# Attention on one Trainium2 core: 128-wide matmuls placed between wide ones, P in two buffers

## The chip, the core and the metric

The kernel runs on one core of one Trainium2 chip. The metric is the device time of one execution in microseconds, median of the runs. The engines have short names here: PE is TensorE's matmul side and PEld its weight loads, DVE is VectorE, ACT is ScalarE, POOL is GpSimd, SP issues DMAs. TensorE's clock has two levels, 1.2 and 2.4 GHz; the granted clock is shown as a share of the upper one.

## The reference, cut to what matters

```python
def attn(x, W_K, W_Q, W_V, W_O):        # x 4 x 512 x 256, 16 heads of 128
    k = einsum('ihd,bpd->biph', W_K, x)
    q = einsum('ihd,bpd->biph', W_Q, x)
    v = einsum('ihd,bpd->biph', W_V, x)
    scores = einsum('biph,biqh->biqp', k, q)
    mask = tril(ones((pos, pos)))
    masked = scores * mask - 1e10 * (1.0 - mask)
    attn = softmax(masked / sqrt(d_head), axis=-1)
    z = einsum('biqp,biph->biqh', attn, v)
    return einsum('df,bqf->bqd', W_O, z_flat)
...
mod = (silu(c) @ wmod).reshape(4, 6, 1, -1)         # sa, ca, ga, sb, cb, gb
h = layernorm(x) * (1 + ca) + sa
x = x + ga * attn(h, ...)
h = layernorm(x) * (1 + cb) + sb
x = x + gb * ffn(h, ...)     # down 256->128, top-2 of 8 experts, shared expert, up, core path
```

The change touches the attention, and of the rest only where the vector gb is kept.

## The kernel before

All is fp32. Nearly every operand of a matmul is kept as two parts in the rounded type fp32r, a high part and a low part, and each product is three matmuls in a row: high by high, high by low, low by high (`mm3`, L631 to L633). Each matmul loads its own 128x128 stationary operand.

The attention is cut into 64 units, one for each batch element and head (`unit(u)`). A unit has these steps on PE. The steps q and k project to 128 x 512, six 512-wide matmuls each. The step v is twelve 256-wide matmuls. S makes the causal scores in twelve matmuls: four row blocks i, each 128(i+1) wide, three matmuls per block. T transposes the ten 128x128 blocks of the normalised scores P on PE (L733). The step z multiplies the transposed P by v in twelve matmuls that are 512, 384, 256 and 128 wide, three of each. The step wo is the output projection, twelve 256-wide matmuls.

Between these steps work the other engines. For S, DVE adds the mask and takes the row minimum of the negated scores (nb, L1034), ACT takes exp into PB and sums rows (L535), DVE takes the reciprocals (ri, L1043), and then ACT scales the last row block (L574) and DVE the other three (L1047, "norm"). For T, ACT copies each bank's transposes to `pth` (L597) and DVE makes the low part `ptl` (L1054); T uses the banks T0, T1 and S2, and z waits until all three low parts are made (`s_pl`). For q, k, v and z, ACT copies the high part (L586) and DVE makes the low part (L1023); their results and wo's go through the three banks M0 to M2 in turn.

One list of steps, `attention_plan()`, sets the order on every engine: each engine walks the same list and does its own share of each step, strictly in that order, so a step's place in the list is its place in ACT's and DVE's queues as well. In the steady part an iteration i is: S(i+1), q(i+2), k(i+2), norm(i+1), wo, z(i), one v, T(i+1). The exps of S(i+1) are split in ACT's queue: those of the first bank stand at S, those of the other two behind the copy of q(i+2). "fill" steps (layer norms, router) are put between. After the attention `ffn_plan()` runs the feed-forward part in the same way; its first gelu, step dn(0), is asked on ACT to wait for the last T (L602), since its result lies where PB was.

Of the kernel before, what the change touches and what calls it, by code (L numbers as in the profile page):

```python
# [13 lines left out]
NU = B * H  # L14
# [33 lines left out]
def attention_plan():  # L48
# [20 lines left out]
    for b in range(2):  # L69
# [14 lines left out]
            ("nm", 0, 0), ("nm", 0, 1), ("mod",),  # L84
            ("h", 0, 0), ("h", 0, 1), ("wh", 2), ("q", 0), ("k", 0), ("v", 0, 0), ("S", 0), ("norm", 0), ("q", 1), ("k", 1), ("v", 0, 1), ("T", 0), ("wh", 3)]
    for i in range(NU):
        steps = list(fill.get(i, []))

        def add(*events):
            for ev in events:  # L90
                plan.append(ev)
                if steps and ev[0] in ("S", "q", "wo", "z", "v", "T"):
                    plan.extend(steps.pop(0))

        if i + 1 < NU:
            add(("S", i + 1))
        if i + 2 < NU:
# [12 lines left out]
        plan += post.get(i, [])  # L110
        if i + 2 == NU:
            plan.append(("dn", 0))
# [85 lines left out]
def build(nc, x, ct, wmod, wat, wfa, wfb, cst, bcol, b2, ub, cb, out, scr, scw):  # L198
# [20 lines left out]
    with ExitStack() as ctx:  # L219
# [12 lines left out]
        cc = sb("cc", C_END)  # L232
        gab = sb("gab", 2048)
        bc = sb("bc", B_END)
# [43 lines left out]
        s_x = [sem(f"s_x{b}") for b in range(B)]  # L278
        s_ct, s_wm, s_wm2, s_c, s_b, s_bc, s_g = (sem(n) for n in ("s_ct", "s_wm", "s_wm2", "s_c", "s_b", "s_bc", "s_g"))
        s_st = [sem("s_st0"), sem("s_st1")]  # L280
# [21 lines left out]
        def bank(ev):  # L302
            return M[use[ev] % 3]

        def hT(b, k):
# [71 lines left out]
        def _(sp):  # L377
# [12 lines left out]
            for ev in plan:  # L390
# [4 lines left out]
                elif ev[0] == "wh":  # L395
# [30 lines left out]
        def _(pool):  # L426
# [7 lines left out]
            for ev in plan:  # L434
# [6 lines left out]
                if ev[0] == "mg":  # L441
# [16 lines left out]
                    pool.wait_ge(s_gd, 32)  # L458
                    flat = scr.rearrange("(o a) b n -> o (a b n)", o=1)
                    pool.dma_start(gab[:], flat.broadcast_to([128, 2048])).then_inc(s_g, 16)  # L460
                if ev[0] == "acc" and ev[2] > 0 and ev not in OWN:
# [36 lines left out]
                if ev[0] == "xb":  # L498
# [5 lines left out]
                    pool.wait_ge(s_xn, 2 * (B + t) + 2)  # L504
                    pool.wait_ge(s_g, 16)
                    pool.tensor_tensor(gob[:], oub[:], g, ALU.mult).then_inc(s_xb, 1)
# [13 lines left out]
        def _(act):  # L520
# [5 lines left out]
            def exps(u, ns):  # L526
                for n in ns:
# [4 lines left out]
                    for i in chunks:  # L532
                        w = 128 * (i + 1)
                        a = S_AT[i][1]
                        ins = act.activation(PB[:, P_OFF[i]:P_OFF[i] + w], PS[bk][:, a:a + w], ACT.Exp,  # L535
                                             bias=nb[:, i:i + 1], scale=-1.0, accum_out=sm[:, i:i + 1])
                    ins.then_inc(s_E, 1)

            for ev in plan:
# [30 lines left out]
                elif kind == "norm":  # L570
                    u = ev[1]
                    act.wait_ge(s_ri, u + 1)
                    p = PB[:, P_OFF[3]:P_OFF[3] + 512]
                    act.activation(p, p, ACT.Copy, scale=ri[:, 3:4]).then_inc(s_P3, 1)  # L574
# [54 lines left out]
        def _(pe):  # L629
            def mm3(o, lhs, rhs, start, stop, **kw):  # L630
                pe.matmul(o, lhs[0], rhs[0], start=start, stop=False, **kw)  # L631
                pe.matmul(o, lhs[0], rhs[1], start=False, stop=False, **kw)  # L632
                return pe.matmul(o, lhs[1], rhs[0], start=False, stop=stop, **kw)  # L633

            pe.wait_ge(s_z, 1)
# [7 lines left out]
            for ev in plan:  # L643
# [42 lines left out]
                elif kind in ("q", "k"):  # L686
# [6 lines left out]
                    for k in range(2):  # L693
                        if k and h == 0:
                            pe.wait_ge(me, use[("h", b, 1)] + 1)
                        ins = mm3(o[:], wt(g % 2, a + 512 * k, 128), hT(b, k), k == 0, k == 1)
                    ins.then_inc(mf, 1)
                elif kind == "v":
# [8 lines left out]
                elif kind == "S":  # L707
# [6 lines left out]
                    for n, (bk, chunks) in enumerate(S_ORDER):  # L714
                        if u > 0:
                            pe.wait_ge(s_E, 3 * u - 3 + n + 1)
                            if bk == 2:
                                pe.wait_ge(s_pl, 3 * u - 2)
                        for i in chunks:
                            a, w = S_AT[i][1], 128 * (i + 1)  # L720
                            ins = mm3(PS[bk][:, a:a + w], lane(q, 128 * i, 128), lane(kk, 0, w), True, True)
                        ins.then_inc(s_S, 1)
                elif kind == "T":
                    u = ev[1]
                    pe.wait_ge(s_N, u + 1)
                    pe.wait_ge(s_P3, u + 1)
                    for n, (bk, chunks) in enumerate(T_ORDER):
                        if u > 0:
                            pe.wait_ge(s_pl, 3 * u - 3 + n + 1)
                        for j in chunks:  # L730
                            a = T_AT[j]
                            for i in range(j, 4):
                                ins = pe.transpose(PT[bk][:, a + 128 * (i - j):a + 128 * (i - j) + 128],  # L733
                                                   PB[:, P_OFF[i] + 128 * j:P_OFF[i] + 128 * j + 128], ident)
                        ins.then_inc(s_T, 1)
                elif kind == "z":
# [4 lines left out]
                    pe.wait_ge(s_pl, 3 * u + 3)  # L741
                    for j in range(4):
                        w = 512 - 128 * j
                        ins = mm3(o[:, 128 * j:512], (vh[:, va + 256 * j:va + 256 * j + 128],
                                                      vl[:, va + 256 * j:va + 256 * j + 128]),
                                  (pth[:, T_OFF[j]:T_OFF[j] + w], ptl[:, T_OFF[j]:T_OFF[j] + w]), j == 0, j == 3)
                    ins.then_inc(mf, 1)
# [102 lines left out]
        def _(v):  # L850
# [81 lines left out]
            for ev in plan:  # L932
# [105 lines left out]
                elif kind == "norm":  # L1038
# [6 lines left out]
                    for i in (1, 0, 2):  # L1045
                        p = PB[:, P_OFF[i]:P_OFF[i] + 128 * (i + 1)]
                        ins = v.tensor_scalar(p, p, ri[:, i:i + 1], None, ALU.mult)  # L1047
# [136 lines left out]
                elif kind == "up":  # L1184
                    _, t, c2 = ev
                    v.wait_ge(mf, use[ev] + 1)
                    if t:
                        v.wait_ge(s_fin, 2 * t - 1 + c2)
                    fbuf = fb[:, 512 * c2:512 * c2 + 512]
                    f = fbuf.rearrange("p (a n) -> p a n", a=2)  # L1190
                    g = gab[:, 1024 + t * 256:1280 + t * 256].rearrange("p (a n) -> p a n", a=1)
                    v.tensor_tensor(f, bank(ev)[:].rearrange("p (a n) -> p a n", a=2), bcast(g, [128, 2, 256]),
                                    ALU.mult).then_inc(me, 1)
# [65 lines left out]
```

## Time and profile before

| | |
|---|---|
| three timed runs | 903.02, 901.08, 902.13 us; median 902.13 |
| span of the profiled execution | 901.1 us |
| PE busy | 872.9 us (97%), 5462 matmuls |
| PEld busy | 781.2 us (87%) |
| DVE, ACT, POOL busy | 76%, 62%, 30% |
| mean granted clock | 0.980 |

The profiled execution is known by its span, the time from the first to the last instruction; nothing is listed outside it. The start of a matmul in a timeline is recorded, its end is modelled: matmuls are pipelined, so their durations overlap and the distance between two starts is the time that one takes of the engine. In brackets behind a row stands how long the engine was idle before it, and on whose result it waited. The chain that ended last lies on PE for 83% of the span.

### The profile page before, as it was taken

What the parts mean: (1) busy time and instruction counts of PE and PEld (TensorE: products, weight loads), DVE (VectorE), ACT (ScalarE), POOL (GpSimd) and SP (SyncE); (2) the same over time, 40 slices, a digit from 0 to 9 for tenths busy, and PEclk for the clock granted to TensorE, in tenths of its full rate; (3) what the DMA queues carried; (4) which work ended last, traced back from release to release, by engine and by line L of the source; (5) the groups of instructions that cost most, each with busy time, mean ns of one, the idle gap of its engine ahead of it and who ended that gap; (6) DMA issues with size and microseconds to landing.
All of it is one profiled execution on the core that took longest, in us unless ns stands there. A gap on an engine that the chain in (4) does not pass through costs nothing.

```text
span 901.1 us, 15397 instructions
## 1 busy us (share of the span) xinstructions
PE 872.9 (97%) x5462; PEld 781.2 (87%) x5462; DVE 689.2 (76%) x1705; ACT 563.0 (62%) x1274; POOL 268.3 (30%) x183
## 2 busy tenths in 40 slices
PE   6999999999999999999999999999999998999996
PEld 6889999999999999999999999999999875777675
DVE  5778887777777777777777777778788979687996
ACT  3655766566566656655665665666656677485772
POOL 3142222211112221111222211232141465577753
PEclk7999999999999999999999999999999999799998
DMA  7120000000000010000000000010000020112130
GB/s 243 47 95 1 24 25 24 24 1 1 2 1 24 24 27 22 1 1 1 25 24 24 24 1 1 24 42 24 2 1 1 26 74 22 58 48 83 47 103 27
DMA packets 10442, 28.63 MB, mean 32 GB/s; under 512 B 1408, under 2 KB 1568, under 8 KB 10112
## 3 DMA queue, kind: packets, MB, share of 16 engines
q1 hardware_dynamic: 9712, 25.80, 9.0%
q0 software_dynamic: 368, 1.34, 0.4%
q8 instruction: 44, 0.72, 0.3%
q10 hardware_dynamic: 288, 0.53, 0.2%
q14 instruction: 30, 0.25, 0.1%
HBM read 25.49 MB, written 2.17 MB: 31 GB/s over the span
## 4 chain that ended last, share of the span: by engine, by line
PE 83%; DVE 7%; issue 3%; ACT 3%; POOL 2%; DMA 1%; POOLq 0%; DVEq 0%; ACTq 0%
PE M L631 18%; PE M L632 18%; PE M L633 18%; PE T L733 6%; PE S L631 6%; PE S L633 5%; PE S L632 5%; DVE Gr L1182 3%; PE S L733 2%; PE T L631 1%; PE T L632 1%; PE T L633 1%; ACT G L623 1%; ACT Gr L625 1%; DMA bc<-in_bcol 1%
## 5 line engine op out<-in xcount | busy, mean ns | idle before, releaser
L489 POOL TENSOR_TENSOR X<-X,fb 128x512 f32<-128x512 f32 x64 | 83.5, 1305 | 521.9 <-DVE fb L1068 521.9
L535 ACT ACTIVATE PB<-S,nb 128x128 f32<-128x128 f32 (+3 forms) x256 | 133.9, 534 | 117.5 <-DVE nb L1034 117.5
L1023 DVE TENSOR_TENSOR qk<-M,qk 128x512 fp32r<-128x512 f32 x128 | 88.4, 692 | 82.2 <-ACT qk L586 82.2
L1034 DVE CUSTOM_DVE_ANT_0 S<-S,cc 128x128 f32<-128x128 f32 (+3 forms) x256 | 117.6, 522 | 0.6 <-PE S L633 0.6
L631 PE MATMUL M<-hh,W 128*128 128x512 f32 x264 | 104.7, 397 | 2.3 <-DVE hl L1010 2.3
L632 PE MATMUL M<-hl,W 128*128 128x512 f32 x264 | 104.1, 394 | 0.0
L633 PE MATMUL M<-hh,W 128*128 128x512 f32 x264 | 103.7, 393 | 0.0
L1182 DVE TENSOR_TENSOR Gr<-G,Gr 128x512 fp32r<-128x512 f32 x84 | 81.0, 972 | 19.7 <-ACT Gr L625 19.1
L631 PE MATMUL S<-qk 128*128 128x128 f32 (+3 forms) x256 | 88.1, 344 | 0.0
L623 ACT ACTIVATE G<-S,bc 128x512 f32<-128x512 f32 x84 | 58.1, 691 | 48.0 <-PE S L633 34.4
L633 PE MATMUL M<-pth,vl 128*128 128x512 f32 (+3 forms) x256 | 82.8, 324 | 0.0
L632 PE MATMUL M<-ptl,vh 128*128 128x512 f32 (+3 forms) x256 | 82.6, 323 | 0.0
L633 PE MATMUL S<-qk 128*128 128x128 f32 (+3 forms) x256 | 82.4, 322 | 0.0
L632 PE MATMUL S<-qk 128*128 128x128 f32 (+3 forms) x256 | 82.2, 321 | 0.0
L1054 DVE TENSOR_TENSOR ptl<-T,pth 128x512 fp32r<-128x512 f32 x128 | 81.9, 681 | 0.1
L586 ACT CAST qk<-M 128x512 fp32r<-128x512 f32 x128 | 76.1, 595 | 7.0 <-PE M L633 7.0
L574 ACT ACTIVATE PB<-PB,ri 128x512 f32<-128x512 f32 x64 | 46.3, 724 | 53.9 <-DVE ri L1043 53.9
L631 PE MATMUL M<-pth,vh 128*128 128x512 f32 (+3 forms) x256 | 79.3, 310 | 0.0
L1023 DVE TENSOR_TENSOR vl<-M,vh 128x512 fp32r<-128x512 f32 x64 | 44.3, 691 | 42.4 <-ACT vh L586 42.2
L631 PE MATMUL M<-W,hh 128*128 128x256 f32 x256 | 75.4, 295 | 0.0
L633 PE MATMUL M<-W,hl 128*128 128x256 f32 x256 | 72.5, 283 | 0.0
L632 PE MATMUL M<-W,hh 128*128 128x256 f32 x256 | 72.3, 282 | 0.0
(186 smaller groups left out, 2484.3 us busy)
## 6 DMA issues: line engine op xcount, KB each, us to landing
stage<-in_wat SPq DMA_DIRECT2D x16, 512.0 KB, 3.9
gab<-scw SPq DMA_DIRECT2D x16, 256.0 KB, 3.3
tmp<-scw SPq DMA_DIRECT2D x16, 256.0 KB, 3.4
X<-in_x SPq DMA_DIRECT2D x4, 512.0 KB, 6.0
stage<-in_wfa SPq DMA_DIRECT2D x3, 512.0 KB, 3.8
out<-X SPq DMA_DIRECT2D x3, 512.0 KB, 2.6
X<-in_wmod SPq DMA_DIRECT2D x1, 1024.0 KB, 7.7
gab<-scr POOLq DMA_DIRECT2D x1, 1024.0 KB, 5.0
```

Source lines behind the costliest of these rows:

```text
L489: pool.tensor_tensor(X[:, a:a + 512], X[:, a:a + 512], fb[:, c2 * 512:c2 * 512 + 512], ALU.add).then_inc(s_y, 1)
L535: ins = act.activation(PB[:, P_OFF[i]:P_OFF[i] + w], PS[bk][:, a:a + w], ACT.Exp, bias=nb[:, i:i + 1], scale=-1.0, accum_out=sm[:, i:i + 1])
L586: act.copy(dst, bank(ev)[:]).then_inc(mh, 1)
L623: act.activation(G32[:, (n % 2) * 512:(n % 2) * 512 + 512], PS[n % 3][:], ACT.Gelu, bias=bias).then_inc(s_v, 1)
L631: pe.matmul(o, lhs[0], rhs[0], start=start, stop=False, **kw)
L632: pe.matmul(o, lhs[0], rhs[1], start=False, stop=False, **kw)
L633: return pe.matmul(o, lhs[1], rhs[0], start=False, stop=stop, **kw)
L733: ins = pe.transpose(PT[bk][:, a + 128 * (i - j):a + 128 * (i - j) + 128], PB[:, P_OFF[i] + 128 * j:P_OFF[i] + 128 * j + 128], ident)
L1023: v.tensor_tensor(lo, bank(ev)[:], hi.bitcast(F32), ALU.subtract).then_inc(me, 1)
L1034: ins = v.tensor_tensor_reduce(PS[bk][:, a:a + w], PS[bk][:, a:a + w], mask[:, 512 - w:512], -INV, BIG, ALU.add, ALU.min, nb[:, i:i + 1])
L1054: v.tensor_tensor(ptl[:, a:z], PT[bk][:, 0:z - a], pth[:, a:z].bitcast(F32), ALU.subtract).then_inc(s_pl, 1)
L1182: v.tensor_tensor(lo, G32[:, (n % 2) * 512:(n % 2) * 512 + 512], hi.bitcast(F32), ALU.subtract).then_inc(s_gl, 1)
```

## The change

Four things are changed in the attention.

1. The ten transposes of unit i no longer stand together. Each of the first five 512-wide matmuls of q(i+2) and of k(i+2) is followed by one of them (`t_step`), in the order bank T0 (4), T1 (4), S2 (2).
2. In S the three products of the 384-wide and the 128-wide block alternate, and in z those of the 512-wide and the 128-wide block. S now starts with bank S2.
3. P has two buffers, by the parity of the unit: PB and a new stretch of `gab`. The vector gb, which was there, is loaded by a DMA of its own after the last T.
4. In the list T(i) stands behind k(i+2) and ahead of norm(i+1), and v now stands ahead of z. ACT's copies and DVE's low parts of T(i) move with it. For the last two units there is no q or k, and T stands in one piece right ahead of z.

```diff
-S_ORDER = [(1, [0, 2]), (0, [3]), (2, [1])]
+S_ORDER = [(2, [1]), (1, [2, 0]), (0, [3])]
-T_ORDER = [(2, [2]), (1, [1, 3]), (0, [0])]
+T_ORDER = [(0, [0]), (1, [1, 3]), (2, [2])]
+T_STEPS = [(bk, j, i) for bk, js in T_ORDER for j in js for i in range(j, 4)]
...
         if i + 2 < NU:
             add(("q", i + 2), ("k", i + 2))
-        if i + 1 < NU:
-            add(("norm", i + 1))
-        if i >= 2:
-            add(("wo", i // 2 - 1, i % 2))
+            add(("T", i), ("norm", i + 1))
+            add(("wo", i // 2 - 1, i % 2)) if i >= 2 else None
+        else:
+            add(("wo", i // 2 - 1, i % 2), ("T", i))
+            add(("norm", i + 1)) if i + 1 < NU else None
         add(*pre.get(i, []))
-        add(("z", i))
         if i + 2 < NU:
             add(("v", i // 2 + 1, i % 2))
-        if i + 1 < NU:
-            add(("T", i + 1))
+        add(("z", i))
...
+        def P_at(u, a, n):
+            return PB[:, a:a + n] if u % 2 == 0 else gab[:, 1024 + a:1024 + a + n]
...
+                elif ev == ("z", NU - 1):
+                    sp.wait_ge(s_gd, 32)
+                    sp.wait_ge(s_T, 3 * NU)
+                    flat = scr[1].rearrange("(o b) n -> o (b n)", o=1)
+                    sp.dma_start(gab[:, 1024:2048], flat.broadcast_to([128, 1024])).then_inc(s_gb, 16)
...
+            def t_step(u, n):
+                bk, j, i = T_STEPS[n]
+                if n == 0:
+                    pe.wait_ge(s_N, u + 1)
+                    pe.wait_ge(s_P3, u + 1)
+                if n in (0, 4, 8) and u > 0:
+                    pe.wait_ge(s_pl, 3 * u - 3 + n // 4 + 1)
+                if n == 8 and u + 1 < NU:
+                    pe.wait_ge(s_E, 3 * (u + 1) + 1)
+                a = T_AT[j] + 128 * (i - j)
+                ins = pe.transpose(PT[bk][:, a:a + 128], P_at(u, P_OFF[i] + 128 * j, 128), ident)
+                if n in (3, 7, 9):
+                    ins.then_inc(s_T, 1)
...
-                        ins = mm3(o[:], wt(g % 2, a + 512 * k, 128), hT(b, k), k == 0, k == 1)
-                    ins.then_inc(mf, 1)
+                        w, h_ = wt(g % 2, a + 512 * k, 128), hT(b, k)
+                        for n, (l, r) in enumerate(((0, 0), (0, 1), (1, 0))):
+                            ins = pe.matmul(o[:], w[l], h_[r], start=(k == 0 and n == 0), stop=(k == 1 and n == 2))
+                            if (k, n) == (1, 2):
+                                ins.then_inc(mf, 1)
+                            if ev[1] >= 2 and 3 * k + n < 5:
+                                t_step(ev[1] - 2, 5 * (kind == "k") + 3 * k + n)
...
+                        for m_, (l, r) in enumerate(((0, 0), (0, 1), (1, 0))):
+                            for i in chunks:
+                                a, w = S_AT[i][1], 128 * (i + 1)
+                                ins = pe.matmul(PS[bk][:, a:a + w], lane(q, 128 * i, 128)[l], lane(kk, 0, w)[r],
...
+                    for n in range(10 if ev[1] + 2 >= NU else 0):
+                        t_step(ev[1], n)
...
+                    for js in ((0, 3), (1,), (2,)):
+                        for m_, (l, r) in enumerate(((vh, pth), (vh, ptl), (vl, pth))):
+                            for j in js:
+                                ins = pe.matmul(o[:, 128 * j:512], l[:, va + 256 * j:va + 256 * j + 128],
```

On PE in the steady part, before: the end of a v (M<-W,hl and the like), the ten transposes (T<-cc,PB), and the start of S (S<-qk). The names are output<-inputs.

```order
L632 MATMUL M<-W,hh 128x256
L633 MATMUL M<-W,hl 128x256
L733 MATMUL S<-cc,PB 128x128 x2
L733 MATMUL T<-cc,PB 128x128 x8
L631 MATMUL S<-qk 128x128
L632 MATMUL S<-qk 128x128
L633 MATMUL S<-qk 128x128
L631 MATMUL S<-qk 128x384
```

After the change, the end of S and the start of q(i+2):

```order
L751 MATMUL S<-qk 128x512 x3
L722 MATMUL M<-hh,W 128x512
L655 MATMUL T<-cc,PB 128x128
L722 MATMUL M<-hl,W 128x512
L655 MATMUL T<-cc,PB 128x128
L722 MATMUL M<-hh,W 128x512
L655 MATMUL T<-cc,PB 128x128
L722 MATMUL M<-hh,W 128x512
```

The transposes left the place ahead of S and stand one by one behind 512-wide matmuls (M<-hh,W and M<-hl,W).

On ACT in the steady part, before: copies of z and v, copies of the transposes (pth), exps of the first bank (PB,sm<-S,nb), copy of q, the other exps, copy of k.

```order
L586 CAST zt<-M 128x512 [waits mf]
L586 CAST vh<-M 128x512 [waits mf]
L597 CAST pth<-S 128x256 [waits s_T]
L597 CAST pth<-T 128x512 [waits s_T] x2
L535 ACTIVATE PB,sm<-S,nb 128x128 [waits s_N,s_M]
L535 ACTIVATE PB,sm<-S,nb 128x384
L586 CAST qk<-M 128x512 [waits mf]
L535 ACTIVATE PB,sm<-S,nb 128x512 [waits s_M]
L535 ACTIVATE PB,sm<-S,nb 128x256 [waits s_M]
L586 CAST qk<-M 128x512 [waits mf]
```

After the change, from the first bank's exp to the copies of the transposes:

```order
L544 ACTIVATE gab,sm<-S,nb 128x256 [waits s_N,s_M]
L595 CAST qk<-M 128x512 [waits mf]
L544 ACTIVATE gab,sm<-S,nb 128x384 [waits s_M]
L544 ACTIVATE gab,sm<-S,nb 128x128
L544 ACTIVATE gab,sm<-S,nb 128x512 [waits s_M]
L595 CAST qk<-M 128x512 [waits mf]
L606 CAST pth<-T 128x512 [waits s_T] x2
L606 CAST pth<-S 128x256 [waits s_T]
L583 ACTIVATE gab<-gab,ri 128x512 [waits s_ri]
```

The copies of the transposes stood between the copy of v and the exps; now they stand behind the copy of k, and the exps behind the copy of q are those of the 384-, 128- and 512-wide blocks.

On ACT at the end of the attention, before: the last T's copies, then the first gelus of the feed-forward part (u, ur), then the copy of the last z.

```order
L586 CAST zt<-M 128x512 [waits mf]
L597 CAST pth<-S 128x256 [waits s_T]
L597 CAST pth<-T 128x512 [waits s_T] x2
L605 ACT_TABLE_LOAD [waits s_T]
L605 ACTIVATE u<-M,bc 128x512 [waits mf]
L607 ACTIVATE ur<-M,bc 128x512
L586 CAST zt<-M 128x512 [waits mf]
```

After the change:

```order
L583 ACTIVATE gab<-gab,ri 128x512 [waits s_ri]
L595 CAST zt<-M 128x512 [waits mf]
L614 ACT_TABLE_LOAD [waits s_T]
L614 ACTIVATE u<-M,bc 128x512 [waits mf]
L616 ACTIVATE ur<-M,bc 128x512
L606 CAST pth<-T 128x512 [waits s_T] x2
L606 CAST pth<-S 128x256 [waits s_T]
L595 CAST zt<-M 128x512 [waits mf]
```

The load of gelu's table, which waits for the last T on PE (s_T), and both gelus now stand ahead of the copies of that T.

## Rows read from the trace of the kernel before

**Rows 1.** Busy time and granted clock (PEclk) by stretch: the attention's steady part.
```profile
205.00:600.00 395.00, 395.00 (x2635) 366.53 (x2634) 288.67 (x754) 243.97 (x609) 74.97 (x49) 1.00 0.05 14
```

**Rows 2.** Timeline of PE over one unit: start, duration in us, operation, shapes.
```profile
303.48 0.30 PE L631 MATMUL S<-qk 128*128 128x128 f32 x1
...
305.48 0.40 PE L631 MATMUL M<-hh,W 128*128 128x512 f32 x1
...
308.22 0.28 PE L631 MATMUL M<-W,zt 128*128 128x256 f32 x1
...
312.87 0.28 PE L633 MATMUL M<-W,hl 128*128 128x256 f32 x1
...
314.00 0.30 PE L631 MATMUL S<-qk 128*128 128x128 f32 x1
```

**Rows 3.** Timeline at the end of z's narrow matmuls: matmuls (PE) and weight loads (PEld).
```profile
311.23 0.19 PEld L632 LDWEIGHTS M<-ptl,vh 128*128 128x128 f32 x1
...
311.45 0.19 PEld L631 LDWEIGHTS M<-W,hh 128*128 128x128 f32 x1
311.51 0.33 PE L631 MATMUL M<-W,hh 128*128 128x256 f32 x1
311.56 0.19 PEld L632 LDWEIGHTS M<-W,hh 128*128 128x128 f32 x1
311.68 0.28 PE L632 MATMUL M<-W,hh 128*128 128x256 f32 x1
```

**Rows 4.** Timeline of PEld: the transposes' loads and the first load of S.
```profile
302.58 0.90 PEld L733 LDWEIGHTS T<-cc,PB 128*128 128x128 f32 x8
303.45 0.19 PEld L631 LDWEIGHTS S<-qk 128*128 128x128 f32 x1
```

**Rows 5.** Timeline around a matmul that waited for DVE.
```profile
104.52 0.69 DVE L1010 TENSOR_TENSOR hl<-fb,hh 128x512 fp32r<-128x512 f32 x1 [0.37 <-ACT hh L569]
...
105.26 0.19 PEld L631 LDWEIGHTS M<-hh,W 128*128 128x128 f32 x1 [0.29 <-DVE hl L1010]
...
105.37 0.19 PEld L632 LDWEIGHTS M<-hl,W 128*128 128x128 f32 x1
105.60 0.40 PE L632 MATMUL M<-hl,W 128*128 128x512 f32 x1
```

**Rows 6.** Timeline of ACT between scores and the copy of q.
```profile
316.84 0.37 ACT L535 ACTIVATE PB<-S,nb 128x128 f32<-128x128 f32 x1 [1.81 <-DVE nb L1034]
...
317.76 0.58 ACT L586 CAST qk<-M 128x512 fp32r<-128x512 f32 x1
318.22 0.71 ACT L535 ACTIVATE PB<-S,nb 128x512 f32<-128x512 f32 x1
...
318.90 0.49 ACT L535 ACTIVATE PB<-S,nb 128x256 f32<-128x256 f32 x1
```

**Rows 7.** Timeline at a hand-over from PE to ACT to DVE.
```profile
323.39 0.28 PE L633 MATMUL M<-W,hl 128*128 128x256 f32 x1
...
323.71 0.59 ACT L586 CAST vh<-M 128x512 fp32r<-128x512 f32 x1 [0.90 <-PE M L633]
...
324.33 0.69 DVE L1023 TENSOR_TENSOR vl<-M,vh 128x512 fp32r<-128x512 f32 x1 [0.79 <-ACT vh L586]
...
324.94 0.41 DVE L1054 TENSOR_TENSOR ptl<-S,pth 128x256 fp32r<-128x256 f32 x1
```

**Rows 8.** Timeline of DVE: evictions of the transposes back to back.
```profile
314.75 1.28 DVE L1054 TENSOR_TENSOR ptl<-T,pth 128x512 fp32r<-128x512 f32 x2
315.94 0.29 DVE L1034 CUSTOM_DVE_ANT_0 S<-S,cc 128x128 f32<-128x128 f32 x1
```

**Rows 9.** Waits of PE: total us, times, longest.
```profile
PE S L733 <- DVE PB L1047: 3.0, 2, 1.6
```

**Rows 10.** Timeline of ACT at the end of the attention.
```profile
707.59 1.28 ACT L605 ACT_TABLE_LOAD   x1
...
709.47 0.68 ACT L607 ACTIVATE ur<-M,bc 128x512 fp32r<-128x512 f32 x1
```

More of the change, by code:

```diff
@@ L84, in attention_plan @@
             ("nm", 0, 0), ("nm", 0, 1), ("mod",),
[L85 removed]
+            ("h", 0, 0), ("h", 0, 1), ("wh", 2), ("q", 0), ("k", 0), ("v", 0, 0), ("S", 0), ("norm", 0), ("q", 1), ("k", 1), ("v", 0, 1), ("wh", 3)]
     for i in range(NU):
@@ L232, in build @@
         cc = sb("cc", C_END)
-        gab = sb("gab", 2048)
+        gab = sb("gab", 1024 + 1280)
         bc = sb("bc", B_END)
@@ L278, in build @@
         s_x = [sem(f"s_x{b}") for b in range(B)]
-        s_ct, s_wm, s_wm2, s_c, s_b, s_bc, s_g = (sem(n) for n in ("s_ct", "s_wm", "s_wm2", "s_c", "s_b", "s_bc", "s_g"))
+        s_ct, s_wm, s_wm2, s_c, s_b, s_bc, s_g, s_gb = (sem(n) for n in ("s_ct", "s_wm", "s_wm2", "s_c", "s_b", "s_bc", "s_g", "s_gb"))
         s_st = [sem("s_st0"), sem("s_st1")]
@@ L458, in _ @@
                     pool.wait_ge(s_gd, 32)
-                    flat = scr.rearrange("(o a) b n -> o (a b n)", o=1)
-                    pool.dma_start(gab[:], flat.broadcast_to([128, 2048])).then_inc(s_g, 16)
+                    flat = scr[0].rearrange("(o b) n -> o (b n)", o=1)
+                    pool.dma_start(gab[:, 0:1024], flat.broadcast_to([128, 1024])).then_inc(s_g, 16)
                 if ev[0] == "acc" and ev[2] > 0 and ev not in OWN:
@@ L504, in _ @@
                     pool.wait_ge(s_xn, 2 * (B + t) + 2)
-                    pool.wait_ge(s_g, 16)
+                    pool.wait_ge(s_gb, 16)
                     pool.tensor_tensor(gob[:], oub[:], g, ALU.mult).then_inc(s_xb, 1)
@@ L534, in exps @@
                         a = S_AT[i][1]
-                        ins = act.activation(PB[:, P_OFF[i]:P_OFF[i] + w], PS[bk][:, a:a + w], ACT.Exp,
+                        ins = act.activation(P_at(u, P_OFF[i], w), PS[bk][:, a:a + w], ACT.Exp,
                                              bias=nb[:, i:i + 1], scale=-1.0, accum_out=sm[:, i:i + 1])
@@ L572, in _ @@
                     act.wait_ge(s_ri, u + 1)
-                    p = PB[:, P_OFF[3]:P_OFF[3] + 512]
+                    p = P_at(u, P_OFF[3], 512)
                     act.activation(p, p, ACT.Copy, scale=ri[:, 3:4]).then_inc(s_P3, 1)
@@ L716, in _ @@
                             pe.wait_ge(s_E, 3 * u - 3 + n + 1)
[L717 to L721, printed above, removed]
+                            if bk == 2 and u > 1:
+                                pe.wait_ge(s_pl, 3 * u - 3)
+                        for m_, (l, r) in enumerate(((0, 0), (0, 1), (1, 0))):
+                            for i in chunks:
+                                a, w = S_AT[i][1], 128 * (i + 1)
+                                ins = pe.matmul(PS[bk][:, a:a + w], lane(q, 128 * i, 128)[l], lane(kk, 0, w)[r],
+                                                start=(m_ == 0 and i == chunks[0]), stop=(m_ == 2),
+                                                skip_group_check=True)
                         ins.then_inc(s_S, 1)
                 elif kind == "T":
[L724 to L735, printed above, removed]
+                    for n in range(10 if ev[1] + 2 >= NU else 0):
+                        t_step(ev[1], n)
                 elif kind == "z":
@@ L741, in _ @@
                     pe.wait_ge(s_pl, 3 * u + 3)
[L742 to L746, printed above, removed]
+                    for js in ((0, 3), (1,), (2,)):
+                        for m_, (l, r) in enumerate(((vh, pth), (vh, ptl), (vl, pth))):
+                            for j in js:
+                                ins = pe.matmul(o[:, 128 * j:512], l[:, va + 256 * j:va + 256 * j + 128],
+                                                r[:, T_OFF[j]:T_OFF[j] + 512 - 128 * j],
+                                                start=(j == 0 and m_ == 0), stop=(j == 2 and m_ == 2),
+                                                skip_group_check=True)
                     ins.then_inc(mf, 1)
@@ L1045, in _ @@
                     for i in (1, 0, 2):
-                        p = PB[:, P_OFF[i]:P_OFF[i] + 128 * (i + 1)]
+                        p = P_at(u, P_OFF[i], 128 * (i + 1))
                         ins = v.tensor_scalar(p, p, ri[:, i:i + 1], None, ALU.mult)
@@ L1191, in _ @@
                     g = gab[:, 1024 + t * 256:1280 + t * 256].rearrange("p (a n) -> p a n", a=1)
+                    if t == 0 and c2 == 0:
+                        v.wait_ge(s_gb, 16)
                     v.tensor_tensor(f, bank(ev)[:].rearrange("p (a n) -> p a n", a=2), bcast(g, [128, 2, 256]),
```

## Prediction

> **What bounds the kernel now.** I looked first at the busy times by stretch. Between 205 and 600 us PE is busy for all 395 us at the full clock [rows 1], and no wait of PE falls in that stretch. So a unit costs what its matmuls take of PE. The timeline of PE then gives the unit: from one S to the next it is 314.00 - 303.48 = 10.52 us [rows 2]. The reader is to take distances between starts there, not durations. A 512-wide matmul takes (308.22 - 305.48)/12 = 0.228 us; from 311.68 [rows 3] to 312.87 [rows 2] are ten 256-wide ones, 0.119 us each.
>
> The 128-wide ones are the special case. Their matmuls would need a quarter of 0.228, but their weight loads start 0.11 us apart (311.23, two later 311.45) [rows 3], and the eight transposes' loads take (303.45 - 302.58)/8 = 0.109 us each [rows 4]. They are bound by the load. What can a wide neighbour hide of that? The end of z tells. The 256-wide matmul behind the narrow ones is recorded at 311.51, and its successor comes at 311.68, 0.17 us later instead of 0.12. The successor's load starts at 311.56. Another case says the same: a 512-wide matmul that had waited has its load at 105.26, the next load at 105.37 and the next matmul at 105.60 [rows 5]. The distance of 0.34 is 0.11 for its own load and 0.23 for its stream. I read from both that a matmul truly begins when its load is through, 0.11 us after it started, and that the next load starts just then and not earlier. Then every matmul costs the longer of its own stream and its successor's load, whatever stands next to it.
>
> **The change on PE.** There are 16 128-wide matmuls in a unit (10 in T, 3 in S, 3 in z). By this rule each costs 0.11 us before and after: alone behind a wide one, its own load was hidden before as well, but the load of the wide one that follows can't start before it does. The gain of the interleaving is nothing. In sum, 18 x 0.228 + 30 x 0.119 + 16 x 0.11, and 6 x 0.174 for the 384-wide ones (halfway between 0.119 and 0.228), make 10.48 us, 0.04 less than the unit takes. It has five places where a narrower matmul is followed by a wider one; if the rest belongs to them they cost at most 0.01 each. The change makes 18 such places of five. I take half of that, 13 x 0.005 = 0.07 us per unit; the bounds are nothing and 0.13. The bound below nothing is the first rival.
>
> **The change in the list.** Before, T(i)'s evictions ran while PE did S, q, k and wo ahead of z(i). Now they stand behind the copy of k(i+2) on ACT, and PE has only wo and v before z(i) asks for the last `ptl`. From the start of k's last matmul PE needs 0.23 + 24 x 0.119 = 3.09 us to reach z. The other side:
> - k's result reaches ACT. For a 256-wide matmul it is 323.71 - 323.39 = 0.32 us from its start; 256 columns more at 2.4 GHz make 0.43 [rows 7].
> - ACT is not free then. Behind the copy of q it does the exps of the two other banks: 318.22 - 317.76 = 0.46 for the copy, 317.76 - 316.84 = 0.92 for 128 and 384, 318.90 - 318.22 = 0.68 for 512, together 2.06 us [rows 6]. k follows q by 6 x 0.228 + 5 x 0.11 = 1.92. So the copy of k is 0.14 late.
> - From ACT's start to DVE's start 0.62, DVE's low part of k 0.61 [rows 7], two `ptl` of 512 columns 315.94 - 314.75 = 1.19 [rows 8], the last, of 256 columns, 0.41 [rows 7]. ACT's three copies keep ahead of DVE, at under 0.5 us each.
> - From the end on DVE to the load on PE 0.05 (104.52 + 0.69 to 105.26), and the load 0.11, now in the open [rows 5].
>
> Sum: 0.43 + 0.14 + 0.62 + 0.61 + 1.19 + 0.41 + 0.05 + 0.11 = 3.56. PE waits 3.56 - 3.09 = 0.47 us ahead of z, in each of the 62 units i = 0 to 61. Behind the waiting z stands the whole queue of PE, and nothing gives it back: the next unit has the same wait. The 0.07 from above comes on top, less 0.02 since it lets k come later: 0.52 x 62 = 32.2 us.
>
> **Both ends.** PE waited twice for the normalised P, 3.0 us together and 1.6 at most: at the first T and at the last [rows 9]. The first goes, as T(0) now stands between q(2) and k(2). At the end T(62) comes after S(63), and its copies behind S(63)'s exps. There was a wait of 1.6 there ahead of T(63), with wo and z (1.43 + 1.9 us) in front; now wo and T (1.43 + 1.1) stand in front, 0.8 us less cover, and behind the exps follow evictions of 0.62 + 1.19 + 0.41 + 0.16 = 2.4 us where the reciprocal and the scalings stood; what those took lies between nothing and 2.4, and I take half, so 1.2 more. I get 1.6 + 0.8 + 1.2 = 3.6 us. The wait of z(63) is new. ACT loads gelu's table only when T(63) is done, and that and both gelus take (709.47 + 0.68) - 707.59 = 2.56 us [rows 10]; then come the copies, 2.4 us to PE, and 0.27 from PE to ACT: 5.2 us. Together 3.6 + 5.2 - 3.0 = +5.8 us. The bounds are +2, if the work of dn and of the feed-forward start gives half of it back, and +12, if the clock drops in such a hole and the next microseconds run at 1.2 GHz.
>
> The other parts I cost at nothing. The second P buffer takes away a wait of the exp for T that was already over, hidden by ACT's idle time. The DMA of gb is issued by SP, where no weight load stands behind it, and is first needed by the output of the feed-forward part's first batch element.
>
> Sum: 901.1 + 32.2 + 5.8 = 939.1 against the profiled span of 901.1. The median run is 1.0 above that span, so 940 us.
>
> **Rivals.**
> 1. The load is hidden after all: a lone narrow matmul costs PE about 0.06 us, 16 x 0.05 = 0.80 us less per unit. For it speaks that in z the first narrow one's successor is recorded early; against it the 0.17 and 0.34 us above. It decides only if the wait of z does not eat it, and it would: q to k shrinks to 1.67, the copy of k is 0.39 late, PE waits 0.72. Net -0.08 per unit, -5 us, and 903 with the ends; 898 if the ends cost 1 us. This is the case that is not slower, and is faster when the ends or the chain are shorter than I think, by 0.1 us of wait in a unit. The Trainium skill speaks for it: "TensorE: Matmul & The Clock Gate", in the part on the array's architectural detail, says that a matmul can begin before its weight load completes, and in the part on the back-to-back issue gap it has about 81 ns for a 128-wide one in a stream with its load. By that figure 16 x 0.029 = 0.46 us per unit would go, an estimate. This trace's 109 ns speaks against it.
> 2. No wait at z: hand-overs are shorter or DVE goes first. Then 901.1 + 62 x 0.07 + 5.8 + 1.0 = 912 us. Against it, the durations are from the same instructions.
> 3. The wait is twice as long, since DVE's and ACT's other work (layer norms, weight splits, POOL's adds) gets in the way, or each switch between transposes and products costs: 0.47 more in each unit, 969 us.
>
> **Numbers.** My forecast has 0.75, for itself 928 to 958 us. Rival 1 has 0.12, of it 0.06 faster, 0.04 the same, 0.02 slower; rival 2 has 0.08; rival 3 has 0.05. Within 0.2% is 900.3 to 903.9 us, about what measurement can tell from no change. So faster 0.06, same 0.04, slower 0.90. The range reaches from 911, to take in rival 2, to 962.
>
> **What would show it.** A unit of about 11.0 us; in the steady part a wait of PE of about 0.45 us ahead of z's first matmul, released by DVE's `ptl`; distances of 0.34 us from one 512-wide matmul over a transpose to the next (0.29 if rival 1 holds); two holes of 3 to 5 us on PE at the end of the attention. A unit under 10.5 us would prove me wrong, whichever step did it.

## The result and the profile after

The changed kernel takes 953.8 us (median of 4 runs, 951.1 to 954.4) against 902.1 us beside it (901.1 to 903.0). The ratio is 1.058, its 95% interval 1.053 to 1.063. The forecast was 940 us, with a range of 911 to 962. It was slower, as forecast, by 52 us where 38 were expected. The profiled execution has a span of 952.3 us against 901.1, so 51.2 us are to be found.

First the page of the kernel after: busy times, and the chain that ended last, by engine.

```profile
PE 896.1 (94%) x5462; PEld 772.2 (81%) x5462; DVE 686.1 (72%) x1705; ACT 564.9 (59%) x1274; POOL 268.7 (28%) x183
...
PE 51%; ACT 21%; DVE 17%; issue 8%; POOL 2%; DMA 1%; POOLq 0%; DVEq 0%; ACTq 0%
```

PE did the same 5462 matmuls, and the chain that was PE for 83% before now runs over ACT and DVE for 38% of the span (10% before). The stretch of [rows 1], with its length first, then the busy time and the instructions of PE, PEld, DVE, ACT and POOL, and the granted clock (1.00) ahead of two figures on DMA:

```profile
205.00:600.00 395.00, 384.92 (x2491) 339.34 (x2490) 272.18 (x721) 228.57 (x573) 65.31 (x44) 1.00 0.04 12
```

PE stands still for 10 of 395 us there, at the full clock. That is by the recorded starts; the weight loads that nothing hides, worked out next, come on top. Where it stands still, the timeline of PE and PEld in one unit shows: the last two matmuls of v, and z's first matmul with its load, which waited.

```profile
516.25 0.28 PE L641 MATMUL M<-W,hh 128*128 128x256 f32 x1
...
516.37 0.28 PE L642 MATMUL M<-W,hl 128*128 128x256 f32 x1
...
516.89 0.30 PEld L767 LDWEIGHTS M<-pth,vh 128*128 128x128 f32 x2 [0.44 <-issue]
...
516.92 0.47 PE L767 MATMUL M<-pth,vh 128*128 128x512 f32 x1 [0.27 <-DVE ptl L1078]
```

Without the wait z would have begun at 516.37 + 0.12 = 516.49. Its load starts at 516.89, and by [rows 5] the matmul truly begins 0.11 later, at 517.00. That is 0.51 us per unit. The eviction queue behind it, ACT first:

```profile
511.87 0.58 ACT L595 CAST qk<-M 128x512 fp32r<-128x512 f32 x1 [1.56 <-PE M L722]
...
513.26 0.70 ACT L544 ACTIVATE gab<-S,nb 128x512 f32<-128x512 f32 x1
...
513.92 0.60 ACT L595 CAST qk<-M 128x512 fp32r<-128x512 f32 x1
514.39 1.11 ACT L606 CAST pth<-T 128x512 fp32r<-128x512 f32 x2
515.34 0.43 ACT L606 CAST pth<-S 128x256 fp32r<-128x256 f32 x1
```

and DVE, with the last `ptl` that z waits for:

```profile
514.56 0.69 DVE L1047 TENSOR_TENSOR qk<-M,qk 128x512 fp32r<-128x512 f32 x1 [1.38 <-ACT qk L595]
515.16 1.28 DVE L1078 TENSOR_TENSOR ptl<-T,pth 128x512 fp32r<-128x512 f32 x2
516.36 0.41 DVE L1078 TENSOR_TENSOR ptl<-S,pth 128x256 fp32r<-128x256 f32 x1
```

ACT is busy without a gap from the copy of q at 511.87 to 515.8; the copy of k comes 2.05 us after q's, 0.09 more than the 1.96 us between the two results (mean over the units, by the starts of the loads). From its start it is 0.64 to DVE, 0.60 for k's low part, 1.20 and 0.41 for the three `ptl`, then 0.12 to the load. This answers to [rows 6 to 8], instruction by instruction.

Then the transposes among the products. PE and PEld over two of them:

```profile
512.27 0.19 PEld L722 LDWEIGHTS M<-hh,W 128*128 128x128 f32 x1
512.29 0.48 PE L722 MATMUL M<-hh,W 128*128 128x512 f32 x1
...
512.40 0.14 PEld L655 LDWEIGHTS T<-cc,PB 128*128 128x128 f32 x1
...
512.61 0.27 PE L655 MATMUL T<-cc,PB 128*128 128x128 f32 x1
512.61 0.19 PEld L722 LDWEIGHTS M<-hh,W 128*128 128x128 f32 x1
512.64 0.48 PE L722 MATMUL M<-hh,W 128*128 128x512 f32 x1
512.75 0.14 PEld L655 LDWEIGHTS S<-cc,PB 128*128 128x128 f32 x1
```

The reader should look at the loads, since the next load starts when a matmul truly begins. From the load at 512.27 to the transpose's load at 512.40 are 0.13 us, from there to the load at 512.61 are 0.21: a transpose and a 512-wide matmul take 0.34 us together. Apart they took 0.109 + 0.228 before [rows 2, 4]. The recorded starts mislead here, as in [rows 3]: the matmul behind a transpose is recorded only 0.03 us after it, long before its own load is through.

The end of the attention shows two long waits of PE:

```profile
743.91 0.87 PE L767 MATMUL M<-pth,vh 128*128 128x512 f32 x2 [3.70 <-DVE ptl L1078]
...
758.16 0.87 PE L767 MATMUL M<-pth,vh 128*128 128x512 f32 x2 [5.63 <-DVE ptl L1078]
```

and ACT between them, with the last T's copies behind gelu's table and both gelus:

```profile
752.60 1.28 ACT L614 ACT_TABLE_LOAD   x1 [4.21 <-PE S L655]
...
754.48 0.68 ACT L616 ACTIVATE ur<-M,bc 128x512 fp32r<-128x512 f32 x1
755.05 1.07 ACT L606 CAST pth<-T 128x512 fp32r<-128x512 f32 x2
755.99 0.40 ACT L606 CAST pth<-S 128x256 fp32r<-128x256 f32 x1
```

The granted clock of the same stretch, and of the one behind it:

```profile
736.00:762.00 26.00, 16.67 (x86) 15.07 (x85) 13.59 (x37) 8.58 (x19) 5.21 (x4) 0.76 0.10 32
762.00:800.00 38.00, 36.31 (x194) 29.30 (x193) 29.32 (x65) 29.48 (x47) 21.34 (x13) 0.98 0.18 56
```

and of two stretches inside it:

```profile
742.70:749.50 6.80, 5.59 (x17) 4.95 (x18) 3.17 (x11) 1.31 (x2) 1.64 (x2) 0.50 0.01 2
756.40:763.10 6.70, 4.94 (x16) 4.39 (x17) 2.04 (x5) 0.59 (x1) 1.26 (x1) 0.50 0.00 0
```

Before, PE had the full clock throughout this part. Now it is granted 0.76 on average over 26 us: the clock drops to the lower level, 1.2 GHz, inside each of the two waits, at 742.7 and at 756.4, and stays there for 6.8 us each time. What that costs can be read from the starts. z(62) and the six 512-wide matmuls behind it take 5.95 us (743.91 to 749.86), where z and six such matmuls took 1.92 + 1.37 before; z(63) takes 3.65 us (758.16 to 761.81) instead of 1.86. Together that is 4.4 us.

At the start of the attention PE waits too:

```profile
33.98 2.17 PE L751 MATMUL S<-qk 128*128 128x256 f32 x12 [0.95 <-DVE qk L1047]
43.20 0.53 PE L767 MATMUL M<-pth,vh 128*128 128x512 f32 x2 [1.68 <-DVE ptl L1078]
56.30 0.53 PE L767 MATMUL M<-pth,vh 128*128 128x512 f32 x2 [1.72 <-DVE ptl L1078]
```

The kernel before had one wait in this stretch:

```profile
55.04 0.44 PE L733 MATMUL S<-cc,PB 128*128 128x128 f32 x2 [1.41 <-DVE PB L1047]
```

The rows of the changed kernel are S(1), z(0) and z(1); the one of the kernel before is T(2), the third T, between S(2) at 45.36 and S(3) at 58.69.

The 51.2 us by place, from the starts of each unit's S in the two traces: 1.7 us up to S(2); 35.3 us from there to S(63), mostly 0.58 us in each unit (11.10 us against 10.52); 13.4 us from S(63) to the first matmul of the feed-forward part; 0.8 us behind it.

Summed over a unit by step (mean over the units from 200 to 600 us, by the starts of the loads), q, k and T took 3.84 us together before and take 3.91 now. S took 1.91 and takes 1.91, z took 1.92 and takes 1.91, and wo 1.41 in both. v, with the wait behind it, took 1.43 and takes 1.95.

### The profile page after: what moved, and what is told of

The parts are those of the page before. It is cut to its first block, busy times and chain, and to the rows that moved or that the text cites. A ratio compares the mean times of both kernels' runs of the same rounds, so it can differ in the third digit from the quotient of the medians.

```text
span 952.3 us, 15399 instructions
## 1 busy us (share of the span) xinstructions
PE 896.1 (94%) x5462; PEld 772.2 (81%) x5462; DVE 686.1 (72%) x1705; ACT 564.9 (59%) x1274; POOL 268.7 (28%) x183
## 4 chain that ended last, share of the span: by engine, by line
PE 51%; ACT 21%; DVE 17%; issue 8%; POOL 2%; DMA 1%; POOLq 0%; DVEq 0%; ACTq 0%
PE M L767 14%; PE S L751 12%; PE M L722 9%; ACT qk L595 7%; DVE ptl L1078 7%; ACT PB L544 5%; ACT gab L544 5%; DVE qk L1047 5%; PE T L655 4%; DVE Gr L1206 2%; PE S L640 1%; PE T L640 1%; PE S L642 1%; PE S L641 1%; PE T L641 1%
## 5 line engine op out<-in xcount | busy, mean ns | idle before, releaser
L751 PE MATMUL S<-qk 128*128 128x256 f32 (+3 forms) x768 | 134.0, 323 | 1.0 <-DVE qk L1047 1.0
L722 PE MATMUL M<-hl,W 128*128 128x512 f32 x256 | 122.8, 480 | 0.0
L722 PEld LDWEIGHTS M<-hh,W 128*128 128x128 f32 x512 | 92.2, 190 | 33.8 <-DVE hl L1034 3.6
L1058 DVE CUSTOM_DVE_ANT_0 S<-S,cc 128x256 f32<-128x256 f32 (+3 forms) x256 | 117.5, 519 | 0.8 <-PE S L751 0.8
L751 PEld LDWEIGHTS S<-qk 128*128 128x128 f32 x768 | 109.6, 189 | 4.8 <-DVE qk L1047 1.2
L544 ACT ACTIVATE gab<-S,nb 128x256 f32<-128x256 f32 (+3 forms) x128 | 66.6, 531 | 41.4 <-DVE nb L1058 41.4
L544 ACT ACTIVATE PB<-S,nb 128x256 f32<-128x256 f32 (+3 forms) x128 | 66.5, 531 | 39.1 <-DVE nb L1058 39.1
L767 PEld LDWEIGHTS M<-pth,vh 128*128 128x128 f32 x256 | 44.1, 192 | 43.8 <-issue 40.9
L767 PE MATMUL M<-pth,vl 128*128 128x512 f32 (+3 forms) x256 | 73.3, 327 | 0.0
L1047 DVE TENSOR_TENSOR zt<-M,zt 128x512 fp32r<-128x512 f32 x64 | 44.2, 691 | 39.0 <-ACT zt L595 39.0
```

Of the source, the lines that this page charges most:

```text
L544: ins = act.activation(P_at(u, P_OFF[i], w), PS[bk][:, a:a + w], ACT.Exp, bias=nb[:, i:i + 1], scale=-1.0, accum_out=sm[:, i:i + 1])
L722: ins = pe.matmul(o[:], w[l], h_[r], start=(k == 0 and n == 0), stop=(k == 1 and n == 2))
L751: ins = pe.matmul(PS[bk][:, a:a + w], lane(q, 128 * i, 128)[l], lane(kk, 0, w)[r], start=(m_ == 0 and i == chunks[0]), stop=(m_ == 2), ski ...
L767: ins = pe.matmul(o[:, 128 * j:512], l[:, va + 256 * j:va + 256 * j + 128], r[:, T_OFF[j]:T_OFF[j] + 512 - 128 * j], start=(j == 0 and m_ ...
L1047: v.tensor_tensor(lo, bank(ev)[:], hi.bitcast(F32), ALU.subtract).then_inc(me, 1)
L1058: ins = v.tensor_tensor_reduce(PS[bk][:, a:a + w], PS[bk][:, a:a + w], mask[:, 512 - w:512], -INV, BIG, ALU.add, ALU.min, nb[:, i:i + 1])
```

## Experiments

Two theories stood against each other. Mine: a 128-wide matmul costs PE the 0.11 us of the next load wherever it stands, so the new order gives nothing, and nearly all the loss is evictions that come too late. The rival: a wide neighbour hides the load, or else the interleaving itself costs half a microsecond and the waits only show where PE is late.

**T's evictions ahead of k's (e1_T_ahead_of_k).**

```diff
-            add(("q", i + 2), ("k", i + 2))
-            add(("T", i), ("norm", i + 1))
+            add(("q", i + 2), ("T", i), ("k", i + 2))
+            add(("norm", i + 1))
```

> The changed kernel, with T(i)'s copies on ACT and low parts on DVE put ahead of k(i+2)'s in the list; PE's order stays. My theory (the 0.58 us that a unit grew by are 0.51 us of waiting ahead of z for evictions that come too late, and 0.06 us of the interleaving itself): the wait goes, a unit takes 10.56 to 10.62 us, and the time is 954 - 62 x 0.51 = 922 us (917 to 927). The rival (the interleaving itself costs PE the half microsecond, and the wait ahead of z only shows where PE is late): a unit stays above 10.9 us and the time above 940 us.

Measured: 949.1 us (948.9 to 950.6), ratio 1.054 (1.050 to 1.058), a unit of 11.04 us. By its numbers this spoke for the rival, and my expectation failed. The waits of PE in the whole run say why (total us, times, longest):

```profile
PE M L767 <- DVE qk L1047: 14.3, 60, 0.8
PE M L767 <- DVE ptl L1078: 11.6, 4, 5.6
```

z no longer waits for `ptl` but for the low part of k (`qk`). Its result goes to the bank of M0 to M2 that k's result was in, three uses earlier, so z needs k's eviction as well. I had the bank rule before me and left this out. ACT's queue had become no shorter: v with the wait behind it takes 1.90 us here, against 1.95 in the changed kernel and 1.43 without a wait.

**The exps behind the copy of k (e8_exps_behind_k).** The kernel above with the end of the list put right (below), and on ACT:

```diff
-                    if kind == "q" and ev[1] >= 2:
+                    if kind == "k" and ev[1] >= 2:
                         exps(ev[1] - 1, [1, 2])
```

> The last kernel (T's evictions ahead of k's, the end put right) with one more move on ACT alone: the exps of the second and third bank stand behind the copy of k(i+2) and no longer behind the copy of q(i+2). In the last kernel z still waited 0.49 us, now for the low part of k, whose bank of M0 to M2 z needs; ACT had 0.46 + 2.06 - 0.46 of exps and 1.22 of the transposes' copies to do in 1.92 us between q and k. My theory (z waits for whatever eviction stands last in ACT's queue behind k, and the queue was too full; PE's own sum is 10.58 us): the wait goes, a unit takes 10.56 to 10.62 us, 939.6 - 62 x 0.47 = 910 us (906 to 915). The rival (the interleaved PE order itself costs the 0.5 us and any eviction will be late): a unit stays above 10.9 us, over 930 us.

Measured: 909.9 us (908.3 to 910.8), ratio 1.009 (1.006 to 1.012). The stretch of [rows 1] and the starts of two S in this kernel:

```profile
205.00:600.00 395.00, 395.00 (x2616) 353.58 (x2615) 284.64 (x749) 250.28 (x612) 71.25 (x47) 1.00 0.05 14
```

```profile
506.97 2.08 PE L754 MATMUL S<-qk 128*128 128x256 f32 x12
...
517.59 2.08 PE L754 MATMUL S<-qk 128*128 128x256 f32 x12
```

PE is busy for all 395 us again, and a unit takes 10.6 us with the order of PE unchanged. This settles it: the half microsecond was the eviction queue, not the interleaving. What the new order of PE costs is 0.07 us (10.59 on average against 10.52).

**The end of the list put right (e3_tail, e4_T_and_tail).** T(62) goes ahead of wo, and T(63) ahead of dn(0), so that its copies precede gelu's table load.

```diff
-            add(("wo", i // 2 - 1, i % 2), ("T", i))
+            if i + 1 < NU:
+                add(("T", i))
+            add(("wo", i // 2 - 1, i % 2))
...
         if i + 2 == NU:
+            plan.append(("T", i + 1))
             plan.append(("dn", 0))
```

> The changed kernel, with only the end of the list altered: T(62) ahead of wo, and T(63) ahead of dn(0) and of the last wo, so that T(63)'s copies stand ahead of gelu's table load on ACT again. My theory (the two waits of 3.7 and 5.6 us at the end, and the half clock behind them, are 12 of the 52 us): the wait ahead of z(63) shrinks from 5.6 to under 1 us and most of the half clock goes, so 954 - 5 - 4 = 945 us (941 to 948). The rival (the feed-forward part waits for something else there and takes the time back): above 950 us.

> The changed kernel with both alterations: T(i)'s evictions ahead of k(i+2)'s, and the end of the list put right. My theory: the two are at different places and add up, 954 - 32 - 9 = 913 us (908 to 918), still slower than the kernel before by the 0.06 us of interleaving in each unit, by the start and by what is left of the waits at the end. The rival (loads are hidden once nothing waits, so that a unit goes under 10.5 us): under 902 us.

Measured: alone 943.0 us (942.8 to 949.3), ratio 1.049 (1.044 to 1.055), 11 us less than the changed kernel; by the traces, 11.4 us less from S(63) to the end. The wait of 5.6 us is gone and the longest left is 2.2 us. Together with T's evictions ahead of k's 939.6 us (938.9 to 940.2), where 913 was expected: the end gives its 9.5 us there too, but the units still take 11.04 us for the reason above.

**Alternation inside S and z alone (e2_sz_only, e12_sz_again).** On the kernel before, the alternation of S's blocks of 384 and 128 (the 384-wide one now comes first) and of z's of 512 and 128. The diff shows z's:

```diff
-                    for j in range(4):
-                        w = 512 - 128 * j
-                        ins = mm3(o[:, 128 * j:512], ...
+                    for js in ((0, 3), (1,), (2,)):
+                        for m_, (l, r) in enumerate(((vh, pth), (vh, ptl), (vl, pth))):
+                            for j in js:
+                                ins = pe.matmul(o[:, 128 * j:512], ...
```

> The kernel before, with only the alternation inside S (384- and 128-wide) and z (512- and 128-wide); the transposes and the list are untouched. My theory (a lone 128-wide matmul costs PE the 0.11 us of the next load, as in a run): 902 us, within 900 to 906. The rival (a wide neighbour hides the load, a lone one costs 0.06 us): 64 x 6 x 0.05 = 19 us less, 883 us.

> The kernel with only the alternation inside S and z once more, in five rounds: it came out at 0.9976 of the kernel before, with an interval that just held 1, and its unit took 10.48 us instead of 10.52. My theory (0.04 us per unit is real): 0.997, interval below 1. The rival (chance): an interval around 1.

Measured: 897.9 us, ratio 0.998 (0.995 to 1.000); again, in five rounds, 897.8 us (896.7 to 900.0), ratio 0.996 (0.995 to 0.998). Hidden loads would have given 883. It is a little faster than the kernel before all the same, and the fastest of the kernels here that compute everything. A unit takes 10.48 us. But S and z are not what got shorter: S takes 1.914 us in both and z 1.921 instead of 1.924; q and k take 2.72 instead of 2.75, v 1.42 instead of 1.43. It is q that got shorter: its six matmuls take 0.231 us each in the kernel before and 0.227 here, k's six take 0.227 in both. The alternation can't be the only cause, since with P's second buffer alone (below) q's take 0.229. The wait of 1.41 us at T(2) is missing in both traces as well, so from S(2) to S(3) it is 12.0 us instead of 13.4. But that wait differs between kernels with the list of the kernel before anyway: it is 0.5 us in the one below that leaves out three matmuls of a run. Why q and v take less is open.

**The transposes alone among wide ones (e7_T_only).** The kernel with the exps behind k, with S and z in runs again, by the same edit backwards.

> The kernel with the exps behind k, with S and z back in runs (no alternation inside S and z; only the transposes stand between the wide matmuls of q and k). My theory (a lone 128-wide matmul costs what one in a run costs, 0.11 us): within 3 us of the kernel with the exps behind k, about 911 us. The rival (a lone one costs 0.06 us): 64 x 6 x 0.05 = 19 us more than that kernel.

Measured: 912.5 us (909.1 to 913.3), ratio 1.011 (1.008 to 1.015); a unit takes 10.61 us against 10.59. Six lone narrow matmuls more or less make 0.02 us, where hidden loads would make 0.30.

**Three narrow matmuls left out, lone and in a run (e5_no_lone, e6_no_run).** z's three 128-wide matmuls are left out, so the last 128 keys' part of z is not computed: once in the kernel with the exps behind k, where each stands between wide ones (the diff), and once in the kernel before, where they stand in a row.

```diff
-                    for js in ((0, 3), (1,), (2,)):
+                    for js in ((0,), (1,), (2,)):
```

> The kernel with the exps behind k, leaving out the three 128-wide matmuls of z, which stand alone between 512-wide ones there; the last 128 keys' part of z is not computed. This weighs three lone narrow matmuls directly. My theory: 64 x 3 x 0.108 = 21 us less than the kernel with the exps behind k. The rival (the wide neighbours hide their loads): 64 x 3 x 0.06 = 11 us less.

> The kernel before, leaving out the same three 128-wide matmuls of z, which stand in a run there; the last 128 keys' part of z is not computed. Both theories: 64 x 3 x 0.11 = 21 us less than the kernel before, 880 us. It is the measure for the loss of three lone ones.

Measured: lone, 889.2 us (888.5 to 890.1) against 909.9 with them, 20.7 us less, which is 0.108 us each (192 of them). In a run, 877.8 us (877.3 to 882.6) against 901.3, 23.5 us less. By the trace, the units shrink by 0.33 us lone and by 0.34 us in a run. This is the most direct measure: a lone 128-wide matmul costs what its successor's load costs.

**Two groups of five transposes (e10_T_groups).**

```diff
-                            if ev[1] >= 2 and 3 * k + n < 5:
-                                t_step(ev[1] - 2, 5 * (kind == "k") + 3 * k + n)
+                            if ev[1] >= 2 and (k, n) == (0, 2):
+                                for s_ in range(5):
+                                    t_step(ev[1] - 2, 5 * (kind == "k") + s_)
```

> The kernel with the exps behind k, with the transposes in two groups of five, behind the third matmul of q and the third of k, instead of one by one behind ten. q, k and T took 3.84 us together in the kernel before and 3.91 in this one. My theory (each lone transpose among products costs about 7 ns for the change between the two kinds, and hides nothing): two changes instead of ten, 3.84 to 3.86 us, 62 x 0.06 = 3.7 us less than with the exps behind k, 906 us. The rival (the transposes cost this wherever they stand between q and k): no change, 910 us. A third (a wide neighbour hides a part of the loads): slower, above 912 us.

Measured: 908.5 us (907.5 to 909.0), ratio 1.008 (1.005 to 1.010). That lies between the 906 of my theory and the 910 of the rival, and the interval is 2 us to either side, so the times can't tell them apart. By the trace a unit takes 10.57 us instead of 10.59, and q, k and T 3.88, between 3.91 and the 3.84 of the kernel before. So less than half of the 0.07 us hangs on the number of changes between transposes and products; the rest is open. In groups the transposes take 0.109 us each, as before the change, and it is the 512-wide matmuls that take more, 0.232 instead of 0.227.

**P's second buffer alone (e9_P_only).** P at `P_at(u, ...)` and gb's own DMA, nothing else.

> The kernel before, with only the second buffer for P and gb's own DMA; PE's order and the list are untouched. My theory (the buffer's wait was over before, so it gives nothing and costs nothing): no difference, 899 to 903 us. The rival (the two P buffers take a wait off ACT that matters, or the later DMA of gb is waited for): more than 2 us to either side.

Measured: 900.9 us (896.9 to 905.8), ratio 0.999 (0.997 to 1.001). No difference clear of the scatter. By its trace a unit takes 10.51 us, and the wait at T(2) is gone.

**wo ahead of T(63) (e11_sz_wo).** Added to the alternation inside S and z:

```diff
+        if i + 2 == NU:
+            add(("wo", i // 2 - 1, 1))
         if i + 1 < NU:
             add(("T", i + 1))
```

> The kernel with only the alternation inside S and z, and the last unit's output projection put ahead of T(63), where PE waits 1.6 us for the normalised P. A candidate that beats both kernels. My theory: wo's 1.41 us fill that wait, and z(63) then waits 0.6 us for T(63)'s evictions: 0.8 us less than without, 897 us. The rival: nothing gained, since z(63) waits for what T(63) no longer does.

Measured: 902.9 us (900.6 to 903.9), ratio 1.001 (0.999 to 1.002), 5 us worse than without. The waits at this place on PE, and DVE at the same time:

```profile
700.27 0.44 PE L738 MATMUL S<-cc,PB 128*128 128x128 f32 x2 [0.17 <-DVE PB L1054]
...
707.33 0.87 PE L750 MATMUL M<-pth,vh 128*128 128x512 f32 x2 [4.36 <-DVE ptl L1061]
```

```profile
703.41 2.24 DVE L1002 TENSOR_SCALAR tmp<-X,mv,rs 128x256 f32<-128x256 f32 x4 [0.61 <-POOL rs L441]
705.58 0.41 DVE L1061 TENSOR_TENSOR ptl<-S,pth 128x256 fp32r<-128x256 f32 x1
705.91 1.27 DVE L1061 TENSOR_TENSOR ptl<-T,pth 128x512 fp32r<-128x512 f32 x2
```

The first wait is down to 0.17 us, but z(63) waits 4.36, not 0.6. The `ptl` stand behind a layer norm step in DVE's queue (2.24 us from 703.41, itself waiting for POOL), with less cover of PE in front. In the kernel with the alternation alone they stand ahead of it (703.58, the layer norm step at 705.11). The list puts the next fill step behind each wo, so the wo that was added drew the layer norm step ahead of T(63). The clock drops in this wait as well, and is at 0.50 until 713.4. A move of 1.4 us on PE moved a queue on another engine into the path: the fault of the change once more, in small.

## Why the prediction came out as it did

**The new order gives PE nothing: right, and shown.** Leaving out lone narrow matmuls saves 0.108 us each, and S and z take the same either way. What the 0.17 and 0.34 us of [rows 3, 5] said holds. Rival 1 is out. The Trainium skill's page "TensorE: Matmul & The Clock Gate" spoke for it, with a begin before the load completes (architectural detail) and about 81 ns for a 128-wide matmul in a stream (back-to-back issue gap). For this kernel's operands the runs don't agree with the 81 ns: by the traces a unit gets shorter by 0.109 us for each lone one left out and by 0.113 for each one of a run. Whether a matmul begins before its load is complete no run shows; that this hides nothing of the load, they do.

**The price of the interleaving: right in size, partly for another reason.** 0.07 us per unit were forecast and 0.07 measured without the wait (10.59 against 10.52). I had put it on places where a wider matmul follows a narrower one, and had taken the size from 0.04 us that my sum left over. But the alternation inside S and z adds such places and costs nothing, and most of the 0.04 lay in q's six matmuls, at 0.231 us each. All of the price lies in q, k and T. A transpose and the 512-wide matmul behind it take 0.345 us on average, where 0.109 + 0.227 would be 0.336: 0.09 us for the ten pairs of a unit. Against the kernel with the alternation alone, whose unit takes 10.48 us, the price of the moved transposes is 0.11. So the agreement with 0.07 is in part luck.

**The wait ahead of z: right, 0.47 forecast and 0.51 measured.** Of the terms, the copy of k was 0.09 late (forecast 0.14, since k came 1.96 us behind q and not 1.92), the hand-over from ACT to DVE took 0.64 (0.62), the low parts took 0.60 + 1.20 + 0.41 (0.61 + 1.19 + 0.41), the hand-over to PE and the load 0.12 + 0.11 (0.05 + 0.11), and PE's cover from k to z was 3.09 us, as forecast. That taking T out of the way would not do, since k's eviction was needed as well, I saw only in the experiment; for the forecast of this change it made no difference. Each unit came out at 0.58 instead of 0.52, 0.06 too low: 62 times, 3.7 us of the 14 that were missed.

**Both ends: +5.8 forecast, about +16 measured (1.7 + 13.4 + 0.8); this term was mis-sized.** It lies above even the upper bound of +12 that I gave it; the measured time is still in the range, since the steady part came out within some 3 us. The two waits themselves came out nearly as worked out, 3.70 for 3.6 and 5.63 for 5.2. Two things were left out. The first is the clock, which drops in both waits: of the 13.4 us from S(63) on, 3.70 + 5.63 - 1.64 = 7.7 are waits, 1.1 is T(62), which now comes after S(63), and 4.6 are left, of which the starts above show 4.4 as matmuls at the lower clock. I had the clock in the upper bound and took nothing for it in the sum. The experiment that mends the end gives 11 us.

The second is the start. By S(2) it is 1.7 us later although T(1), 1.1 us, no longer stands ahead of S(2), so 2.8 us were lost, and 0.95 + 1.68 of them are the waits of S(1) and z(0). The 1.4 us of gain that I had booked for the first T did not come either. I had misread its place: T(0) and T(1) never waited, the wait was at T(2). It is gone, but z(1) waits 1.72 us in its place: from S(2) to S(3) are 13.73 us against 13.36. z(0) and z(1) wait for the same evictions as in the steady part; why more than 0.51 us there, no run shows.

**The second buffer: right.** Alone it makes no difference.

Rival 2, no wait, is what the kernel with the exps behind k became: 912 us worked out, 909.9 measured. The two don't count the same: the 912 had 5.8 us for the ends, and in that kernel the end is mended, and by the same sum without them it would have been 906; its trace loses 0.8 us up to S(2) and 2.7 us from S(63) on. Rival 3 did not come.

## What to carry to other kernels

Where PE is bound by weight loads, ask what each matmul's successor has to load: the sum of the longer of stream and next load does not depend on the order as long as all loads are equally long, so alternating narrow and wide ones buys nothing where the profile shows loads starting only when the matmul before them begins. When a step moves in a list that all engines follow, work out the queue of the evicting engines at the new place, up to everything the next step waits for, the accumulation bank it reuses included. A mended queue on ACT was worth 30 us here, the whole new order of PE at most a few tenths of a per cent.

## What the runs showed that I had not expected

- The alternation inside S and z makes the kernel 0.4% faster (0.996, 0.995 to 0.998), by shorter q, k and v (2.72 for 2.75 us, 1.42 for 1.43), not by S or z, and without the wait at T(2).
- The clock fell inside waits of 3.7 and 5.6 us, and PE ran at the lower level for some microseconds behind them: 0.76 granted over 26 us, 4.4 us lost. Where the longest wait was 1.6 us, in the kernel before, the same part had the full clock.
- A transpose between fp32r products lets its own load start 0.13 us before the next and shortens the distance to the one after to 0.21; the pair costs 0.345 us instead of 0.336. The recorded start of the matmul behind it, 0.03 us later, is no sign of an early begin.
